# The expert stage of a four-layer kernel: first places made by products, row-wise router logits, and a reordered head norm

## What is computed

```python
# layer 1: gated attention without softmax; its output h is normed per head
h_norm = (h - mean) * jax.lax.rsqrt(var + 1e-05) * outnorm_scale      # 4 heads of 64 per row
# layer 4: mixture of experts, 2 groups of T = 1024 rows, E = 8, capacity C = 160, K = 2 chosen
router_probs = jax.nn.softmax(x @ w_router)
gate, idx = jax.lax.top_k(router_probs, K)
pos = cumsum(one_hot choices over k, then rows) * mask - 1            # a row's place in its expert
dispatch = one_hot(pos, C) * mask                                     # places >= C are dropped
expert_in = jnp.einsum('gtec,gth->egch', dispatch, x)
y = combine(relu(expert_in @ wi) @ wo)
```

## Time and profile before

| | us |
|---|---|
| median of three executions | 591.28 (590.52 to 592.04) |
| the profiled execution | 594.54 |
| its span, first to last instruction | 592.8 |
| PE / DVE / ACT / POOL busy | 519.8 / 381.6 / 327.0 / 142.5 |
| mean granted TensorE clock | 0.952 |

### The profile page before, as it was taken

The page is one execution under the profiler, slowest core; times in us unless marked ns, Lnnn a source line. Parts: engine busy times, 40 slices in busy tenths (PEclk is TensorE's granted clock), DMA queues, the critical chain, the costliest instruction groups (busy, mean ns, idle before and its releaser), DMA issues.

```text
span 592.8 us, 9394 instructions
## 1 busy us (share of the span) xinstructions
PE 519.8 (88%) x3362; PEld 372.6 (63%) x3362; DVE 381.6 (64%) x980; ACT 327.0 (55%) x697; POOL 142.5 (24%) x202
## 2 busy tenths in 40 slices
PE   1989996899999700999999999998999999999994
PEld 1568864654444300887757678777788777677773
DVE  6576889845389989788688699987732232233101
ACT  2857577723389969680389799997122212211220
POOL 2006544000000000000332232211245344534441
PEclk9989999999999955699999999999799999999998
DMA  7910000000000000016000011014215645353410
GB/s 221 305 19 1 2 1 0 2 0 1 0 0 1 1 0 0 1 46 239 2 0 2 1 39 36 2 37 159 52 46 170 200 132 195 121 181 124 132 46 22
DMA packets 32013, 37.62 MB, mean 63 GB/s; under 512 B 8672, under 2 KB 27744, under 8 KB 31968
## 3 DMA queue, kind: packets, MB, share of 16 engines
q1 hardware_dynamic: 28896, 29.07, 15.3%
q0 software_dynamic: 3072, 7.95, 4.3%
HBM read 30.14 MB, written 6.88 MB: 62 GB/s over the span
## 4 chain that ended last, share of the span: by engine, by line
PE 71%; DVE 14%; ACT 9%; issue 2%; POOL 2%; POOLq 0%; DVEq 0%
PE pA L2203 12%; PE pB L2233 10%; PE pC L1869 6%; PE pC L1908 5%; PE pA L1902 3%; PE pB L1918 3%; PE pC L2217 3%; PE pA L1824 2%; PE pB L1824 2%; PE pC L1824 2%; ACT XIT L748 2%; DVE am L1259 2%; DVE arena L1255 2%; PE pB L1998 2%; DVE am L1225 2%
## 5 line engine op out<-in xcount | busy, mean ns | idle before, releaser
L499 POOL TENSOR_TENSOR arena<-KT,par 128x256 f32<-128x256 f32 x32 | 19.0, 615 | 248.6 <-DVE XIT L1333 186.7
L2203 PE MATMUL pA<-arena 128*128 128x320 f32 (+2 forms) x320 | 75.7, 387 | 0.5 <-ACT arena L923 0.5
L937 ACT ACTIVATE arena<-pA 128x320 f32<-128x320 f32 (+2 forms) x80 | 30.7, 384 | 73.0 <-PE pA L2203 67.5
L2203 PEld LDWEIGHTS pA<-arena 128*128 128x128 f32 x320 | 53.7, 190 | 16.2 <-issue 1.1
L2233 PE MATMUL pB<-arena 128*128 128x256 f32 x256 | 59.8, 385 | 0.0
L2233 PEld LDWEIGHTS pB<-arena 128*128 128x128 f32 x256 | 47.2, 190 | 8.5 <-issue 2.3
L1225 DVE TENSOR_REDUCE am<-arena 128x1 f32<-128x512 f32 x48 | 32.1, 682 | 23.0 <-ACT arena L688 22.9
L1869 PE MATMUL pC<-wdnT,XIT 128*128 128x256 f32 x192 | 43.5, 384 | 0.8 <-DVE XIT L1333 0.8
L1409 DVE TENSOR_REDUCE rm<-pA 128x16 f32<-128x2048 f32 x16 | 36.7, 2291 | 8.8 <-PE pA L1902 8.8
L1869 PEld LDWEIGHTS pC<-wdnT,XIT 128*128 128x128 f32 x192 | 36.5, 193 | 6.9 <-DVE XIT L1333 1.6
L1908 PE MATMUL pC<-ident,arena 128*128 128x128 f32 x240 | 35.4, 280 | 1.5 <-ACT XIT L784 0.8
(11 more groups left out here) (338 smaller groups left out, 1147.2 us busy)
## 6 DMA issues: line engine op xcount, KB each, us to landing
arena<-in_L_ffn_wi SPq DMA_DIRECT2D x8, 1024.0 KB, 5.2
arena<-in_L_ffn_wo SPq DMA_DIRECT2D x8, 1024.0 KB
X<-in_x SPq DMA_DIRECT2D x4, 512.0 KB, 5.7
arena<-in_ctx SPq DMA_DIRECT2D x4, 512.0 KB, 7.3
out<-X SPq DMA_DIRECT2D x4, 512.0 KB, 2.9
token_rows<-arena SPq DMA_DIRECT2D x4, 512.0 KB, 4.7
arena<-in_L_ffn_w_up SPq DMA_DIRECT2D x1, 768.0 KB, 7.5
arena<-in_L_ffn_w_gate SPq DMA_DIRECT2D x1, 768.0 KB, 9.2
```

What stands on the lines that cost most here:

```text
L937: nc.scalar.activation(HT[:, e % 2, f, n], ps[2 + f % 2][:, 0:n.stop - n.start], ACT.Relu).then_inc(s["h_relu"], 1)
L2203: last = mm(ps[2 + f % 2][:, 0:n.stop - n.start], WI[:, u, k, f * P:(f + 1) * P], XET[:, u, k, n], start=(k == 0), stop=(k == KD - 1))
```

## The change

1. **First expert's first places by products.** Pass 0 no longer needs a gather for its rows: `select_full(e)` on DVE writes the selection of group 0 in float32 for experts 0 and 1 (8 comparisons of 128 x 192 each), and `e_select(0)` on PE multiplies the rows with it: 2 products of 128 x 128 for each of 8 blocks. POOL still gathers pass 0's rows, for their gate values. The row numbers of passes 0 and 1 (`e_tokens`, `e_places`) move into `e_hidden(0)`; `e_turn(1)`, `count(1)` and `e_tokens(2)` into `e_out(0)`. The `keep_busy` products between are gone.
2. **Logits by position.** All 16 blocks go by `d_row`: 0 to 7 right behind `d_turn(3)`, 8 to 11 behind `d_turn(5)`, 12 and 13 behind `d_turn(7)`, 14 and 15 behind `e_select(0)`. The wide form, its copies and its transposes back are gone. The scale of the last four blocks (`last_rows_scale`) moves on DVE from ahead of the logits to behind `less_largest(0)`.
3. **Head norm.** `head_scale(0)` goes ahead of the two last `w_round`; ACT does all four heads of blocks 0 to 12; `keys(2)` stands behind the last `head_norm`; `values_kept(1)` and `(2)` are done at steps 4 and 9 of the loop and not at 6 and 14.

The core of the diff:

```diff
+        ALL_HEADS = 13
...
-                if b >= HB:
+                if b >= ALL_HEADS:
...
-                if b == 13:
-                    keys(2)
+            keys(2)
             rsqrt(4, NB)
...
+                if t == NB // 2:
+                    head_scale(0)
                 for b in (2 * t - 2, 2 * t - 1):
                     if b >= 0:
                         w_round(b)
-                if t == NB // 2:
-                    head_scale(0)
...
-                if t in (6, 14):
-                    values_kept(1 + t // 14)
+                if t == 4:
+                    values_kept(1)
+                if t == 9:
+                    values_kept(2)
...
+            def select_full(e):
+                for b in range(TG):
+                    V_.tensor_scalar(SELF[e][:, b, :], cidx_f[:, 0, :], place[:, 0, e, b:b + 1], None, ALU.is_equal).then_inc(s["sel_full"], 1)
...
-            logits_0()
+            logits(0)
             largest(0)
             less_largest(0)
+            last_rows_scale()
             link(choose(0, 0))
...
             find_places(0)
-            select(0, 0)
-            logits_1()
+            select_full(0)
+            select_full(1)
+            logits(1)
             digits_kept(0)
...
             d_turn(3)
-            d_logits()
+            for b in range(TG):
+                d_row(b)
             d_turn(4)
-            d_back()
+            keep_busy(ps[7], 2)
             d_turn(5)
-            keep_busy(ps[7], 2)
-            d_logits4()
+            for b in range(TG, 12):
+                d_row(b)
             keep_busy(ps[7], 3)
-            d_back4()
-            keep_busy(ps[7], 4)
...
+            def e_select(i):
+                pe.wait_ge(s["d_xt"], 7)
+                for b in range(TG):
+                    pe.wait_ge(s["sel_full"], b + 1)
+                    for k in range(KD):
+                        last = mm(ps[k][:, 0:P], XR[:, b, k * P:(k + 1) * P], SELF[i][:, b, 0:P], start=(b == 0), stop=(b == TG - 1))
+                last.then_inc(s["xe_tr"], 1)
...
             d_turn(6)
-            keep_busy(ps[7], 2)
+            keep_busy(ps[7], 3)
             d_turn(7)
+            d_row(12)
+            d_row(13)
+            keep_busy(ps[7], 4)
             count(0)
-            for b in range(12, NB):
-                d_row(b)
-            e_tokens(0)
-            e_places(0)
-            keep_busy(ps[4], 6)
-            e_tokens(1)
-            keep_busy(ps[4], 2)
-            e_places(1)
-            keep_busy(ps[4], 6)
-            count(1)
-            e_turn(0)
+            e_select(0)
+            d_row(14)
+            d_row(15)
             for i in range(len(PASSES)):
```

More of the change, by code:

```diff
@@ L649, in head_norm @@
                 act.wait_ge(s["head_stat"], 1 + b // HB)
-                for n in range(NH0 if b < HB else NH0 - 1):
+                for n in range(NH0 if b < ALL_HEADS else NH0 - 1):
                     last = nc.scalar.activation(at(HU, b)[:, n, 0:DH0], at(HU, b)[:, n, 0:DH0], ACT.Identity, scale=rstd[:, cols(b * NH0 + n, 1)], bias=s2[:, cols(b * NH0 + n, 1)])
@@ L901, in _ @@
             norm4_act(8)
-            lt_copy()
+            rsqrt(9, 4, 12)
             norm4_act(9)
-            rsqrt(9, 4, 12)
             xt4(4)
             xt4(5)
-            lt4_copy()
             act.wait_ge(s["xr_ready"], 5)
@@ L922, in xet @@
                 if part == "A":
[L923 removed]
+                    src = ps[1][:, 0:2 * P].rearrange("p (k n) -> p k n", k=KD) if i else pA[:, 0:2, 0:P]
+                    nc.scalar.activation(XET[:, u, :, 0:P], src, ACT.Copy).then_inc(s["xet_ready"], 1)
                     return
@@ L935, in relu @@
                 for f in range(NFT):
+                    if i == 0 and f == 5:
+                        exp4(1)
                     act.wait_ge(s["h_done"], i * NFT + f + 1)
@@ L1587, in _ @@
             less_largest(1)
+            link(choose(1, 0))
             number(0)
-            select(1, 0)
-            link(choose(1, 0))
             chosen_off(1)
+            largest(1)
             digits_kept(1)
-            second(1)
+            choose(1, 1).then_inc(s["oh_ready"], 1)
             number(1)
@@ L1599, in _ @@
             select(0, 1)
+            select(1, 1)
+            digits_kept(2)
             gate_column(0)
-            digits_kept(2)
-            select(1, 1)
             number(2)
@@ L2186, in e_hidden @@
                 for f in range(NFT):
+                    if i == 0 and f == 1:
+                        e_tokens(0)
                     if i == 0 and f == 4:
-                        e_tokens(2)
+                        e_places(0)
+                    if i == 0 and f == 6:
+                        e_tokens(1)
+                    if i == 0 and f == 7:
+                        e_places(1)
+                    if i == 1 and f == 1:
+                        e_places(2)
                     if i == 2 and f == 4:
@@ L2227, in e_out @@
                         if part == "A":
-                            if i == 0 and f == 1:
-                                e_places(2)
-                            if (i, f) in ((0, 4), (1, 6)):
-                                e_turn(i + 1)
+                            if i == 0 and f == 3:
+                                count(1)
+                            if i == 0 and f == 7:
+                                e_tokens(2)
+                                e_turn(1)
+                            if i == 1 and f == 6:
+                                e_turn(2)
                             pe.wait_ge(s["h_relu"], i * NFT + f + 1)
```

83 lines of the change are left out of this document (28 added, 55 removed).

## The result

The changed kernel takes 595.44 us (median of five, 594.34 to 595.89), the kernel before, run on the same chip, 591.98 us (five, 590.52 to 592.45). The ratio is 1.0046, interval 1.0025 to 1.0066: **slower by 0.5%**, 2.7 us by the ratio, 3.5 between the medians. The forecast was +6.8 us and 598.0. The side was right, the size was 2 to 2.5 times too large.

What follows compares the result with a forecast made beforehand. PE was taken to bound the kernel, almost alone from 425 us on. Head norm -1.1, router +5.4, gather +2.0 and second clock fall +0.5 gave +6.8 us: 598.1 on the median of 591.3, say 598.0; range 590 to 604.

Steps and rivals of the forecast that it cites:

- count(0) at 422: Router: PE's queue of row-wise logits, turns and fillers, mostly at the low clock, delays count(0) to 422 us.
- e_select ... I take 5.8: Router: the 32 entries of e_select take 5.8 us, between 3.5 at the high clock and 7.6 at the low.
- e_hidden(0) starts at 430.5: End of the router: the first expert starts at 430.5 us against 425.08 before.
- the term +5.4: Router up to the first expert: e_hidden(0) starts 5.4 us later than before.
- D: Rival, router: the clock falls but row-wise products don't stretch; count(0) at 420.5, 596.5 us in all; chance 0.10.
- case A: Rival, router: clock holds and the gather's pause doesn't cost it; e_hidden(0) at 421.8, 588.9 us in all, faster; chance 0.12.
- C: Rival, router: the clock falls, but the fillers bring it back before count(0); 591.6 to 594.1 us in all; chance 0.14.
- +2.0 at the gather of pass 1: First to second expert: PE waits for pass 1's gathered rows inside e_out(0); 10.5 us instead of 8.5.
- +0.5 for a second fall in that pause: Pass 1: the clock may fall again in PE's pause of about 1.5 us; +0.5 us, bounds 0 and +3.
- -1.1 for the head norm: Head norm: values_kept(2) leaves the gap between DVE's last blocks, so the loop ends 1.1 us sooner; bounds -0.2 and -1.6.
- Passes 1 to 9 do the same work as before: Expert passes behind e_hidden(1): no further change in time was expected, so the sum had no term.
- the same 3.2 us: Conversion from profiled execution to median: 3.2 us lower, so 601.3 became 598.1.

Runs made afterwards that it cites:

- b_experts: The changed kernel with the head norm as before, so parts 1 and 2 alone; 596.91 us, ratio 1.0069 to the kernel before.
- n_after: The changed kernel itself, profiled and timed again for its third trace; 595.20 us, ratio 1.0025 to the kernel before.
- d_nofill: The changed kernel without the 12 keep_busy products in the router; ratio 1.0070 to the kernel before.
- e_early: The changed kernel with count(0) right behind d_row(11), e_select(0) ahead of d_row(12) to (15), and 2 of 12 keep_busy products left; ratio 1.0028.
- j_rows: The changed kernel with unread products inside e_hidden of passes 4 to 8: 8, 16, 32 and 64 of 8 columns, 16 of 128; 643.3 us, one execution.
- c_wide: The changed kernel with the router's logits the wide way as before, parts 1 and 3 kept; 593.96 us, ratio 1.0020 to the kernel before.
- l_best: Kernel with parts 1 and 3, wide logits, expert 1's numbers first, e_turn(1) ahead of e_tokens(2), e_turn(2) two products earlier; 590.66 us, ratio 0.9938.
- h_swap: The changed kernel with expert 1's numbers made before expert 0's and e_turn(1) ahead of e_tokens(2); 596.28 us, ratio 1.0064 to the kernel before.
- g_after: The changed kernel itself, profiled and timed again for its second trace; 597.03 us, ratio 1.0063 to the kernel before.
- m_mixed: The changed kernel with 16 unread 8-column products in each of passes 4 to 8, each followed by a 128-column one in 7 and 8; 625.26 us, one execution.

## Why the prediction was right or wrong

**The step that failed** is "count(0) at 422" and what hung on it, "e_select ... I take 5.8" and "e_hidden(0) starts at 430.5": the term +5.4. It let the clock stay low from the first rows until the middle of `e_select`. The three traces of the changed kernel had it low for 10.2, 3.4 and 6.8 us, `count(0)` 15.5, 12.3 and 12.3 us behind the free point and not 16.8, and `e_hidden(0)` 21.4, 18.1 and 19.7 behind it where 19.8 was before. With the four other traces of that code the term measures **-3.2 to +1.5**, -0.8 on average, not +5.4. It misses by 3.9 us in the first trace and by 6.2 on average; the next largest parts of the first trace's difference that the sum had wrong are 1.3 (at 240 us) and 1.0 (ahead of the stage). The prices inside it were good: 0.114 us a row-wise entry, nearly twice that at the low level, which refutes D (and with it, as a price for such products, the load time at a fixed clock of the Trainium skill's page "TensorE: Matmul & The Clock Gate", section "LDWEIGHTS (loading the stationary operand)"), and `e_select` 3.8 at the high level, 5.4 and 5.9 where the level changed within. With the clock held the router of case A came out in b_experts; its time, 588.9, did not, and not only because b_experts leaves out the head norm: the wait ahead of `e_hidden(2)` was in no case. What was wrong was to take one course of the clock for a property of the program, and the longest one at that. The rows of before show one execution; A (b_experts) and C (the first trace of the changed kernel) both came out of the same code, and the forecast's course, low through all of `e_select`'s first half, came only in part, in n_after, d_nofill and e_early (`e_select` over 5.44, 5.89 and 5.10 us).

The evidence that I took for the fall was ambiguous. The earlier trace rows shows the clock falling behind 16 row-wise entries *and* a pause of half a microsecond. In j_rows 16 entries alone did nothing, and in c_wide and l_best the same 16 without the pauses did nothing. That 32 in a row can bring it down was right, and is shown now, not argued.

**+2.0 at the gather of pass 1: right.** 10.7 us between the first two experts against 8.5, and 10.6 to 10.8 in every trace with its order of numbers but e_early's 10.5; forecast 10.5. The cause is that named only in part. PE did stop for the rows inside `e_out(0)`, but for 0.41 us, and for 0.52 ahead of `e_tokens(2)`, not for 1.5 at once; and h_swap, where the rows are there in time, still needs 9.9. So the late gather is worth 0.8 of the 2.2 us. The other 1.4 are the products moved into `e_hidden(0)` and `e_out(0)` and a pause of 0.32 that is left in h_swap.

**+0.5 for a second fall in that pause: wrong here, right elsewhere.** The clock read 1.00 at pass 1 in every trace. It did fall right behind a pause in n_after (behind `count(0)`) and in b_experts (ahead of `e_hidden(2)`).

**-1.1 for the head norm: right** in the mechanism, and near in size: 0.9 at `moments(4)` in every trace, 0.6 by the means at the gate's products, inside the bounds of 0.2 and 1.6. The sum had no term for the clock's return at 240 us, another 1.1 in the traces (1.3 in the first); that the head norm's order caused it was not tried apart, it only goes with it in all thirteen traces.

**"Passes 1 to 9 do the same work as before": wrong.** `e_hidden(1)` to `e_hidden(2)` takes 9.6 to 9.7 us and not 9.2, with `e_places(2)` and `e_tokens(3)` now closer together in `e_hidden(1)` (whether that is the cause was not tried), and 11.1 to 11.4 in the seven traces in which ACT's copy started late. There the copy begins 1.9 us behind the transposes that it waits for, and the trace names nothing but "remote" as its releaser. This is ACT in the second and the first trace of the changed kernel:

```profile
442.58 0.55 ACT L923 ACTIVATE arena<-pA 128x192 f32<-128x192 f32 x2 [4.77 <-remote]
```
```profile
443.35 0.55 ACT L923 ACTIVATE arena<-pA 128x192 f32<-128x192 f32 x2 [3.09 <-PE pA L2167]
```

What makes it late stays open. It was there in all seven traces with part 1 on two of the chips (b_experts, c_wide and d_nofill on one; g_after, h_swap, e_early and j_rows on the other), in none of the three on a third (n_after, m_mixed, l_best), and not in the first trace of the changed kernel, whose chip isn't on record. So l_best's earlier `e_turn(2)` was not tried against it. The changed kernel has the ratio 1.0063 on a chip with the wait and 1.0025 on the one without, which fits a cost of 1.4 us, but the two intervals overlap.

**The sum for the first trace:** -1.0 (ahead of the stage) -0.5 (head norm) -1.3 (240 us) +1.5 (router) +2.2 (to pass 1) +0.5 (pass 1) = +1.4; measured 1.4. The medians differ by more, 3.5 us, since the profiled execution of before lies 2.6 us above its median and that of after 0.5 above its own. The forecast had been moved from the one to the other by subtracting the same 3.2 us; that is right only if both traces have the same luck with the clock. No execution of the kernel before at a mean clock of 0.965, its best, was traced, so how much of its 2.6 us lies in the router stays open.

The range, 590 to 604, holds the measured 595.4. It was wide because of the clock, and rightly so, but its far end was worked out with the clock low through `e_select`, which no trace shows (and adds up to 604.7, not 604.5). That the measured side is the forecast one is in part luck: the forecast's course of the clock didn't come, the router alone was faster than before in four of seven traces by 1.7 us or more, and a good part of what made the kernel slower lies behind `e_hidden(0)`.

## What to carry to other kernels

- TensorE products with a few columns can bring its clock down although the profile shows the engine busy; watch the granted clock behind such groups, not the busy time. Wide products between them held it here but cost as much again as the narrow ones; the wide form, with its copy and transposes back, gave the shorter router here (16.3 us to the first expert, against 19.1 on average) although its clock fell as well, in three of four traces.
- Where a step of a sum hangs on the granted clock, take two or three traces of the same kernel before believing one: here the same instructions needed 16.6 to 21.4 us.
- The gather that was taken off the first pass was waited for at the next one here. Count from the event that releases the *next* transfer, and move that event first.

## What the runs showed of the hardware

- 32 float32 entries of 8 columns in a row brought the clock to 0.50 in two of three places of one trace (m_mixed) and in the one place of another (j_rows). There 16 didn't and 32 of 128 columns didn't; in m_mixed pairs of both kinds held it at 1.00. PE's busy share was full each time.
- At the low level an entry of 8 columns takes 0.21 us, at the high one 0.114: it follows the clock although only 8 columns move.
- The clock also fell right behind pauses of PE of 1.09 us (n_after, 415.65) and 1.52 us (b_experts, 445.0), and not behind the like pauses in the traces where it was up.
- Executions of one program differ by 3 to 6 us (before: 591.65 to 596.54), with the mean granted clock going from 0.965 to 0.951.
